# h split by GpSimd and transposed by one DMA a batch, statistics of the first residual from accumulating calls, and a new order of calls

## What is computed

```python
x = layernorm(x + causal_attention(x))            # q, k of width 16; values are x itself
x = layernorm(x + x @ ternary(W0).T * scale)
x = layernorm(x + channel_attention(x))           # x3 is the sum inside this layernorm
# mixture of experts, top 1 of 8, and one shared expert; weights ternary times a row scale
h = (x - mean) / sqrt(var + eps) * gamma + beta
shared = silu(h @ sw1.T) @ sw2.T
probs = softmax(h @ router.T); e = argmax(probs)
out = layernorm(x + shared + max(probs) * (silu(h @ ew1[e].T) @ ew2[e].T))
```

## Time and profile before

| | us |
|---|---|
| median of 3 timed runs | 806.72 |
| lowest, highest | 802.95, 810.37 |
| span of the profiled execution | 794.0 |
| median less span | 12.7 |
| PE busy in the span | 721.3 |
| DVE busy | 699.8 |
| ACT busy | 656.5 |
| POOL busy | 335.0 |

### The profile page before, as it was taken

One profiled execution on the slowest core, in us unless ns is written; L12 is line 12 of the kernel. 1 busy time (PEld: TensorE's weight loads), 2 busy tenths in 40 slices (PEclk: granted clock), 3 DMA queues, 4 the chain that ended last, 5 costly groups with the idle time before them and its releaser, 6 DMA issues.

```text
span 794.0 us, 18530 instructions
## 1 busy us (share of the span) xinstructions
PE 721.3 (91%) x5417; PEld 546.5 (69%) x5417; DVE 699.8 (88%) x2124; ACT 656.5 (83%) x1447; POOL 335.0 (42%) x370
## 2 busy tenths in 40 slices
PE   3769998999999999999999999999989977988882
PEld 2556686777767767776776777777777766777771
DVE  5767888899989999998999999999899988998885
ACT  2265759997997998799799789988899976999994
POOL 3000011124334343342523335354567775876667
PEclk9979999999999999999999999999999998999996
DMA  8104301123132131213223023021624447455430
GB/s 264 35 15 119 106 2 55 34 90 98 55 107 70 55 129 43 80 61 108 87 61 114 29 80 108 14 88 41 211 71 149 145 152 206 147 177 163 136 119 30
DMA packets 57217, 76.51 MB, mean 96 GB/s; under 512 B 15453, under 2 KB 37919, under 8 KB 57120
## 3 DMA queue, kind: packets, MB, share of 16 engines
q1 hardware_dynamic: 46016, 48.45, 21.5%
q0 software_dynamic: 9600, 25.25, 8.9%
q10 hardware_dynamic: 1504, 1.64, 0.6%
HBM read 47.42 MB, written 28.91 MB: 96 GB/s over the span
## 4 chain that ended last, share of the span: by engine, by line
PE 67%; DVE 9%; ACT 8%; issue 7%; POOL 3%; DMA 3%; SPq 1%; ACTq 1%; DVEq 0%; POOLq 0%
PE bank L677 9%; PE bank L902 6%; PE bank L889 5%; PE bank L758 4%; PE bank L770 4%; PE bank L626 3%; PE bank L760 3%; PE bank L759 3%; ACT G_S L1845 3%; PE bank L1112 2%; POOL out L4113 2%; PE bank L705 2%; PE bank L716 2%; PE bank L706 2%; PE bank L855 2%
## 5 line engine op out<-in xcount | busy, mean ns | idle before, releaser
L4008 POOL TENSOR_TENSOR R<-rstd,mhalf 128x4 f32<-128x4 f32 x16 | 19.2, 1199 | 261.8 <-DVE rstd L2268 261.8
L4113 POOL DMA_INDIRECT out<-G_y,Gid x72 | 81.7, 1135 | 45.6 <-ACT G_y L1866 24.6
L1845 ACT ACTIVATE G_S<-bank,e1b,e1s 128x256 f32<-128x256 f32 (+1 forms) x188 | 87.1, 580 | 5.9 <-PE bank L1095 5.8
L1112 PE MATMUL bank<-E2T,split 128*128 x576 | 74.6, 284 | 14.5 <-DVE split L3053 11.9
L677 PE MATMUL bank<-X,PT 128*128 128x257 f32 x320 | 83.5, 401 | 0.5 <-ACT PT L1574 0.4
L1095 PE MATMUL bank<-G_T,E1T 128*128 128x256 f16 (+1 forms) x752 | 75.6, 251 | 7.8 <-issue 6.4
L4052 POOL DMA_INDIRECT rrec<-R,pos x64 | 67.8, 1060 | 30.7 <-issue 22.5
L1112 PEld LDWEIGHTS bank<-E2T,split 128*128 128x128 f16 x576 | 56.5, 101 | 27.4 <-issue 18.4
L4043 POOL DMA_INDIRECT hrec<-HN,pos x64 | 67.1, 1049 | 16.7 <-issue 15.9
L1095 PEld LDWEIGHTS bank<-G_T,E1T 128*128 x752 | 60.5, 99 | 17.9 <-issue 10.7
L677 PEld LDWEIGHTS bank<-X,PT 128*128 128x128 f32 x320 | 60.1, 200 | 10.5 <-issue 1.4
(11 more groups left out here) (438 smaller groups left out, 2292.8 us busy)
## 6 DMA issues: line engine op xcount, KB each, us to landing
XT<-in_xT SPq DMA_DIRECT2D x16, 512.0 KB, 4.0
X<-in_x SPq DMA_DIRECT2D x16, 512.0 KB, 6.0
G_h<-hrec SPq DMA_DIRECT2D x25, 257.0 KB, 3.5
G_r<-rrec SPq DMA_DIRECT2D x25, 257.0 KB, 3.4
e1n<-in_ew SPq DMA_DIRECT2D x8, 512.0 KB
e2n<-in_ew SPq DMA_DIRECT2D x8, 512.0 KB, 3.5
G_h<-hrec SPq DMA_DIRECT2D x22, 128.5 KB, 2.4
G_r<-rrec SPq DMA_DIRECT2D x22, 128.5 KB, 2.5
```

Source lines behind the costliest of these rows:

```text
L1112: last = pe.matmul(down_bank(w)[:, j * D:(j + 1) * D], x[w % NGB][:, f, j * P:(j + 1) * P], E2T[:, expert_of[w, j], f, :], start=k == 0, s ...
L1845: last = act.activation(G_S[w % NGS][:, ff, a:b], bk[:, o + a:o + b], ACT.Silu, bias=e1b[:, e, ff], scale=e1s[:, e, ff])
L4113: pool.indirect_dma_start(t["out"], bass.IndirectOffsetOnAxis(Gid[w % NGI][:, j:j + 1], 0), G_y[w % NGY][:, j, :], None, bounds_check=TOK ...
```

## The change

The float32 HN with its transposes on PE is replaced by a float16 pair. Per batch: `hg` (DVE, 4 calls) multiplies x3 by the reciprocal deviation and gamma in one instruction, `hh` (ACT, one call of 1024 elements a partition) rounds to float16, `hl` (POOL, one call) writes the remainder, and `htr` (SP) issues one transposing DMA from SBUF to SBUF of all 16 blocks of 128x128. The record in `hrec` becomes the float16 pair (1024 bytes instead of 1028), so that a group is fetched by a transposing DMA straight into the operand (ring of 8); the token's number moves to `rrec`.

```diff
-HREC, RREC = D + 1, D + 1
+HREC, RREC = 2 * D, D + 2
-NGR, NGB, NGS, NGY, NGI = 5, 4, 3, 4, 8
+NGR, NGH, NGB, NGS, NGY, NGI = 5, 8, 4, 3, 4, 8
+        def htr(b):
+            sp.wait_ge(s["hl"], at("hl", b))
+            if b >= 2:
+                sp.wait_ge(s["up"], at("up", b - 2, 3))
+            sp.dma_start_transpose(HT[b % 2][:].rearrange("p j x c n -> p (j x c) n"),
+                                   HN[b % 2][:].rearrange("p j x d -> p (j x d)")).then_inc(s[f"hTd{b % 2}"], 16)
         def gload(w):
-            if w >= NGR:
-                sp.wait_ge(s["gTr"], at("gTr", w - NGR))
-                sp.wait_ge(s["gid"], w - NGR + 1)
+            if w >= NGH:
+                sp.wait_ge(s["gup"], at("gup", w - NGH, FC - 1))
-                sp.dma_start(G_h[w % NGR][:], hrec[bass.DynSlice(o, SLOT), :].rearrange("(p j) c -> p j c", p=P)).then_inc(s[f"gath{w % NGR}"], 16)
+                sp.dma_start_transpose(G_T[w % NGH][:].rearrange("p x c n -> p (x c) n"), hrec[bass.DynSlice(o, SLOT), :]).then_inc(s[f"gath{w % NGH}"], 16)
         def logits(b):
-            pe.wait_ge(s["HTl"], at("HTl", b, 1))
+            pe.wait_ge(s[f"hTd{b % 2}"], 16 * (b // 2 + 1))
         def x1c(b, j):
-            act.wait_ge(s["mv0"], NT * b + j + 1)
-            act.activation(X1[:, j, :], X1[:, j, :], ACT.Identity, bias=mv[0][:, j, 0:1], scale=-1.0).then_inc(s["x1c"], 1)
+            act.wait_ge(s["x1"], at("x1", b, j))
+            act.activation(X1[:, j, :], X1[:, j, :], ACT.Identity, bias=SM1[b % 2][:, j:j + 1], scale=-float(D)).then_inc(s["x1c"], 1)
+        def sq1(b, j):
+            act.wait_ge(s["x1c"], at("x1c", b, j))
...
+            act.activation(junk1[:, j % 2, :], X1[:, j, :], ACT.Square, scale=D ** -0.5, accum_out=SQ1[b % 2][:, j:j + 1]).then_inc(s["sq1"], 1)
+        def hh(b):
+            act.wait_ge(s["hg"], at("hg", b, 3))
+            if b >= 2:
+                act.wait_ge(s[f"hrec{b % 2}"], 16 * NT * (b // 2))
+                act.wait_ge(s[f"hTd{b % 2}"], 16 * (b // 2))
...
+            act.activation(HN[b % 2][:, :, 0, :], HG[:], ACT.Copy).then_inc(s["hh"], 1)
         def x1(b, i):
-                                     ALU.mult, ALU.subtract).then_inc(s["x1"], 1)
+                                     ALU.mult, ALU.subtract, accum_out=SM1[b % 2][:, i:i + 1]).then_inc(s["x1"], 1)
+        def hg(b, j):
+            if j == 0:
+                dve.wait_ge(s["rs2"], b + 1)
+                if b >= 1:
+                    dve.wait_ge(s["hl"], at("hl", b - 1))
+            dve.scalar_tensor_tensor(HG[:, j, :], X2[b % NX2][:, j, :], R3[b % 4][:, 0, j:j + 1], gamr[:], ALU.mult, ALU.mult).then_inc(s["hg"], 1)
+        def hl(b):
+            pool.wait_ge(s["hh"], at("hh", b))
+            pool.tensor_tensor(HN[b % 2][:, :, 1, :], HG[:], HN[b % 2][:, :, 0, :], ALU.subtract).then_inc(s["hl"], 1)
```

```diff
         load_small()
+        load_tiny()
         load_x(1)
         load_e1(1)
-        load_tiny()
...
         for g in range(2, 8):
-            load_xT(2 * g)
-            load_x(2 * g - 1)
-            load_x(2 * g)
-            maxima(2 * g - 1)
-            one_e2(g - 2)
-            load_xT(2 * g + 1)
-            maxima(2 * g)
-            one_e1(g - 1)
+            htr(2 * g - 5)
+            load_x(2 * g - 1)
+            maxima(2 * g - 1)
+            load_xT(2 * g)
+            one_e2(g - 2)
+            load_x(2 * g)
+            htr(2 * g - 4)
+            maxima(2 * g)
+            load_xT(2 * g + 1)
+            one_e1(g - 1)
```

More of the change, by code:

```diff
@@ L598, in sp_program @@
         row_of = {}
-        for w in range(NEARLY):
-            gload(w)
-            if w < NGR:
-                rload(w)
-            elif w > NGR:
-                rload(w - 1)
-        rload(NEARLY - 1)
+        gload(0)
+        rload(0)
+        gload(1)
+        rload(1)
+        gload(2)
+        rload(2)
+        gload(3)
+        rload(3)
+        gload(4)
+        rload(4)
+        gload(5)
+        gload(6)
+        gload(7)
+        htr(14)
+        htr(15)
+        gload(8)
+        rload(5)
+        gload(9)
+        rload(6)
+        gload(10)
+        rload(7)
+        gload(11)
+        rload(8)
+        gload(12)
+        rload(9)
+        gload(13)
+        rload(10)
+        rload(11)
+        rload(12)
+        rload(13)
         for w in range(NEARLY, NG + 4):
@@ L848, in hT @@
             elif b < B - 1:
-                pe.wait_ge(s["y"], at("y", b - 1, (3, 1)[k]))
-            elif k == 0:
+                pe.wait_ge(s["y"], at("y", b - 1, 3))
+            else:
                 pe.wait_ge(s["place"], at("place", b - 1, 0))
-            else:
-                pe.wait_ge(s["HTl"], at("HTl", b - 1, 1))
-            for j in range(NT):
-                last = pe.transpose(banks[6 + k][:, j * P:(j + 1) * P], HN[b % 2][:, j, k * P:(k + 1) * P], ident[:])
-            last.then_inc(s["hT"], 1)
-        def logits(b):
-            if not 0 <= b < B:
-                return
-            pe.wait_ge(s["HTl"], at("HTl", b, 1))
             W3 = 4 * NE
@@ L1805, in act_program @@
         act.wait_ge(s["vset"], 4)
-        def gT(w):
-            if not 0 <= w < NG:
-                return
-            act.wait_ge(s["gTr"], at("gTr", w))
-            if w >= NGB:
-                act.wait_ge(s["gup"], at("gup", w - NGB, FC - 1))
-            for c in range(DC):
-                last = act.activation(G_T[w % NGB][:, 0, c, :], tr_bank(w)[:, c * SLOT:(c + 1) * SLOT], ACT.Copy, scale=gamc[:, c:c + 1])
-            last.then_inc(s["gT"], 1)
         expert_of = {}
@@ L1871, in act_program @@
         nmr_(0)
+        map_E0(0)
+        exp(0, 0)
         W0T_()
-        for i in range(4):
-            exp(0, i)
+        exp(0, 1)
+        exp(0, 2)
+        exp(0, 3)
+        x1c(0, 0)
         map_r1(0)
-        for i in range(3):
-            x1c(0, i)
+        x1c(0, 1)
+        x1c(0, 2)
+        x1c(0, 3)
+        T1h_(0, 0)
         qk(1)
-        x1c(0, 3)
-        map_E0(0)
-        T1h_(0, 0)
+        T1h_(0, 1)
+        sq1(0, 0)
+        sq1(0, 1)
         map_s(0)
-        T1h_(0, 1)
-        map_E1(0)
+        sq1(0, 2)
+        sq1(0, 3)
         map_r0(1)
@@ L4184, in pool_program @@
         rsc(12, 3)
         hsc(13, 3)
-        power2(14)
-        hid(15)
-        gid_(4)
-        rsc(13, 0)
+        hl(14)
+        power2(15)
+        hid(14)
+        gid_(1)
+        hl(15)
+        gpower(0)
+        gpower(1)
+        gpower(2)
+        scatter(0, 0)
+        hsc(14, 0)
+        rsc(13, 0)
+        rsc(13, 1)
+        scatter(0, 1)
+        rsc(13, 2)
+        rsc(13, 3)
+        scatter(1, 0)
+        gid_(2)
+        gpower(3)
+        gid_(3)
+        gid_(4)
+        hsc(14, 1)
@@ L4190, in pool_program @@
+        scatter(1, 1)
+        scatter(2, 0)
+        hsc(14, 2)
+        hsc(14, 3)
+        scatter(2, 1)
+        rsc(14, 0)
+        gpower(4)
+        scatter(3, 0)
+        hsc(15, 0)
+        scatter(4, 0)
+        hsc(15, 1)
+        scatter(3, 1)
         gid_(5)
         gid_(6)
-        for i in range(1, 4):
-            rsc(13, i)
-        power2(15)
-        gpower(0)
-        for i in range(3):
-            hsc(14, i)
-        gid_(7)
-        hsc(14, 3)
-        gpower(1)
-        scatter(0, 0)
```

1903 lines of the change are left out of this document (886 added, 1017 removed), and 2 rows, old and new, of the table names.

## The result

The changed kernel takes 828.38 us (median of 4 runs, 825.87 to 834.52) beside 805.74 us of the kernel before (802.95 to 810.37): a ratio of 1.0243, interval 1.0197 to 1.029. It is slower, by 2.0 to 2.9%, where 3.2% faster was forecast.

The account below looks back on a forecast made before the run. It took PE as the bound from 120 to 540 us, a mixture to 680, ACT after; -10.4 - 1 - 3 - 5.5 - 2 - 6.5 + 3 = -25.4 from a 794.0 us span gave 768.6, plus 12.7: 781 us (773 to 790, chance 0.45; whole range 762 to 822).

Parts of the forecast that it names:

- Who waits behind these waits: Loop: maxima queued behind htr on SP, hg on DVE, hl's 37 us on POOL; called covered, with +3 us held back.
- the reserve of 3: Loop: +3 us held back for waits of the new way of h left uncovered now and then.
- Transposes from PE: 120 to 540 us: 26 hT calls leave PE at 0.40 us each, -10.4 us, and 1 us of PE idle goes.
- The start: Start: loads ahead of X and e1 end rest_gate's wait, part of x1c's goes too; 3 us won, bounds 0 and 4.7.
- 580 to 680 us: Last batches, sorting and groups together: work leaves DVE, ACT and PE; 5.5 us won, bounds -5 and 13.
- Late groups: 680 to 707 us, groups of one expert: 2 us won; 707 to 762 us, groups of two halves: 6.5 us won.
- rival (1): POOL and the fetches hold the late stages: 14 us less won, 795 us; chance 0.22 together with (5).
- The prices: Per batch: hl 2.3 us, hh 1.2, each hg 0.43, accumulator readout taken as 0, transposing DMA 5 from issue to landing.
- (2): Loop: the transposing DMA is late for logits and maxima, 43 us over twelve batches, 824 us; chance 0.15.
- (3): Loop: the 16 blocks of a transpose follow one another, 30 us each transpose, near 1060 us; chance 0.03.
- (4): The new order also closes PE's pauses of 580 to 680 us, 10 more, loop DMA hidden, 3 more: 768 us; chance 0.15.
- (5): Accumulating x1 or hl costs far more than priced, logits late on even batches, 10 us: 791 us; chance 0.22 with (1).

Follow-up runs that it names:

- e5: The changed kernel with POOL's row of seven scatters broken: the fifth waits for the odd batch's rank product; 804.86 us beside 810.43 of the kernel before.
- e14: The kernel of e5, one wait after four scatters, timed in rounds against the kernel before: ratio 0.9949 (0.9923 to 0.9976), 12 executions.
- e16: The kernel of e5 with two more POOL waits, breaking the row of eight scatters at the first groups: ratio to the kernel before 0.9977 (0.9955 to 0.9999).
- e18: The kernel before, unchanged, profiled a second time, at the upper level: 811.61 us, span 810.1.
- e17: The kernel before with the tiny loads alone issued ahead of X of batch 1: ratio to the kernel before 0.9949 (0.9926 to 0.9973).
- e15: The kernel of e5 with the copy of each group's row numbers moved from POOL to DVE: ratio to the kernel before 0.9972 (0.9946 to 0.9997).
- e12: The kernel of e5 with some 0.3 us more POOL work in each group from the 12th on: 810.64 us beside 804.33 of the kernel before.
- e9: The changed kernel with each batch's transposing DMA replaced by a plain DMA of the same bytes, transposition left out: 819.98 us beside 804.33 of the kernel before.
- e13: The kernel before with three scatters of each even batch's h moved ahead of POOL's next power, making a row of seven: 822.59 us beside 810.58.

## Why the prediction was wrong

**The step that failed** is the paragraph "Who waits behind these waits". It weighed hl's 37 us on POOL, "covered in the loop", and never the order of POOL's scatters, which the change rewrites as well; they were counted at nothing, because POOL is busy 148 of 420 us. At the upper level that order costs far more than the reserve of 3: e5, one wait that breaks the row, takes 5.6 us off beside its kernel before, where the changed kernel stood 22.6 above its own. A part of the failure could not be read from the trace given: it is of the lower level, where such signals aren't late. But the 12.7 us between its span and the median, which I added at the end as a constant, was the sign that something in the timed runs was missing from the profile: the execution of the changed kernel that was profiled took 825.87 us with a span of 824.6, so what lies around the span is 1.3 us.

The row explains about half of the miss. The forecast was 25 us less, the result 23 more; with the row broken e14 is still only 4.8 less. The other 20 us lie in the terms.

**The terms.** Transposes from PE, -10.4 and -1. The same five pairs, in the first profile of the kernel before and in e16, both at the lower level:

```profile
120.22:455.73 335.51, 332.33 (x2350) 244.17 (x2349) 308.88 (x954) 293.59 (x665) 113.86 (x104) 1.00 0.24 75
```

```profile
113.22:449.69 336.47, 328.48 (x2277) 238.84 (x2277) 298.49 (x937) 289.02 (x698) 138.05 (x113) 1.00 0.31 91
```

PE's busy time falls by 3.9 us for 20 calls of `hT`, 0.19 us a call where 0.40 was priced, and its idle time grows from 3.2 to 8.0. Even with nothing late the loop gave nothing back (+1.0), not 11. "PE's work is the time" was too simple for PE at 99%: PE now waits, up to 1.4 us at a time, for the maxima (3.8 us in 120 to 540 us), and for DVE. e16 has waits of its own on POOL, and the changed kernel itself wasn't profiled at the lower level, so how much they hide is open. The reserve of 3 for the maxima was near: 4.8 us of waits in the changed kernel, none over 1.5.

The start, -3, came out at -3.5 against e18, whose batch 4 begins at 117.02; against the first profile (120.22) it is -7, so its size is known to 3 us only. e17 begins batch 4 at 114.36, and its 4 us fit the term.

580 to 680 us, -5.5: +3.1 from the first group to the 16th addition, and +5.1 in the stretch ahead of it, which had no term.

Late groups, -2 and -6.5: -4.3. The groups of two halves fell from 5.5 to 4.82 us, but those of one expert rose from 4.56 to 4.82, with POOL's calls end to end, as rival (1) feared. A part of that is work that the prediction took as unchanged: the two scatters of a late group take 1.96 + 1.54 us instead of 1.43 + 0.98; for the first of them the last section shows beside what. But e15, where POOL had room again, kept 4.80, and e12 shows that more of POOL's work costs at once. So the step seems to be held by a chain that runs through POOL and not by POOL's load; which chain is open.

**The prices.** hl 2.3: 2.20. hh 1.2: 1.06. hg 0.43: 0.42. Reading out x1's accumulator 0 to 0.1: 0.08. The transposing DMA 5: a median of 5.0 from issue to landing, of the eight whose landing the profile tells.

```profile
L3932 POOL TENSOR_TENSOR HN<-HG,HN 128x1024 f16<-128x1024 f32 x16 | 35.1, 2195 | 36.8 <-ACT HN L1679 36.8
...
L1679 ACT ACTIVATE HN<-HG 128x1024 f16<-128x1024 f32 x16 | 16.9, 1057 | 5.6 <-DVE HG L2356 5.0
...
L2266 DVE DVE_READ_ACCUMULATOR X<-bank,RI,X 128x1 f32 x64 | 5.3, 82 | 0.0
```

```profile
HT<-HN SPq DMA_TRANSPOSE x16, 5.0
```

**The rivals.** (2) named a time, 824 us, close to what came, and that was luck: its mechanism is wrong, since in the changed kernel PE never waits for the transposed h. (3) fell with it, and (4) with the loop. Of (5) nothing came: `hl` and the accumulators cost what was priced. Of the Trainium skill, page "Advanced Engine Details and Errata", section X-Bar Transpose (TRN2), the trace agrees with the rule that a transposing DMA is as fast as an ordinary one (in e16, where all sixteen landings are told, 3.6 to 5.4 us, median 3.8, beside a median of 5.0 for a load of X of the same 512 KB). My list of what would prove me wrong had the late maxima and the clock under 0.93 in the groups (0.90 came), but no line on PE's signals.

## What to carry to other kernels

An instruction that is moved costs nothing only when its engine's neighbours are indifferent to it: look at what runs beside a re-ordered queue, not only at whether its engine has room. Where waits end on signals long after the matmuls they belong to, look for a row of indirect scatters on GpSimd and try a wait in it on something that happens a few us later. And when a profile's span stands well below the timed median, profile again before building a sum on it.

## What the hardware showed that was not expected

- At the upper level PE's signals begin to come late some 3 to 4 us after the first scatter of a row begins, about its third or fourth, and are in order again about 1 to 1.8 us behind its last. In the loop the lag reached 5.2 us beside a row of seven (`up` in e9) and 1.7 beside a row of four. While the row runs, late signals come about 1.4 us apart (in the odd batch shown DVE, ACT and DVE are released at 373.52, 374.95 and 376.37), and what is still owed then comes almost at once (in e13 four signals within 0.2 us, from 369.82 on). PE's records meanwhile look normal, and in the changed kernel and e18 the signals of DVE and ACT are on time. It is the same with a plain DMA, with four-byte elements, with another buffer, and in both kernels. What in the chip does it, and why one occasion and the first profile are free of it, is open.
- A pause of 4.3 us on PE was followed by some 3 us at a granted clock of 0.50, which is 1.2 of 2.4 GHz.
- The scatter of a group's rows takes 1.96 us when it starts just behind DVE's split (128x1024, 1.28 us long), and 0.98 when it starts just ahead of it. In e14 it starts 0.17 us behind the split and ends 0.85 us behind the split's end; in the kernel before it starts 0.27 us ahead. POOL and DVE in e14, then in the kernel before:

```profile
744.66 1.96 POOL L4025 DMA_INDIRECT out<-G_y,Gid  x1 [0.16 <-POOL Gid L4011]
...
744.49 1.28 DVE L2992 SCALAR_TENSOR_TENSOR split<-G_S,sdn,split 128x1024 f16<-128x1024 f32 x1
```

```profile
687.74 0.98 POOL L4113 DMA_INDIRECT out<-G_y,Gid  x1 [0.48 <-issue]
...
688.01 1.28 DVE L3053 SCALAR_TENSOR_TENSOR split<-G_S,sdn,split 128x1024 f16<-128x1024 f32 x1
```

By a rule of the Trainium skill, page "DMA: Bandwidth & Descriptors", section SWDGE vs HWDGE vs iDMA, GpSimd writes its descriptors where VectorE locks it out in one of its fast modes. The trace fits that where the split runs first, but it doesn't tell in which mode the split ran, and no run took the split away.
